# Handing five of the last fifteen pieces of a weighted sum to ScalarE and GpSimd, with one release per buffer and a last store in four parts

## What is computed

```python
topw, topi = jax.lax.top_k(scores, K)                 # K = 2 of E = 8 experts
for e in range(E):
    m = topi == e
    sel = m.any(axis=-1)
    wmean = (topw * m).sum() / jnp.maximum(cnt, 1)    # one weight per expert
    y = _mlp(xf, expert_gate_w[e], expert_up_w[e], expert_down_w[e])
    out = out + jnp.where(sel[:, None], y * wmean, 0)
out = out + _mlp(x, shared_gate_w, shared_up_w, shared_down_w)
x = x + out
```

## Time and profile before

| | |
|---|---|
| median of 3 executions | 1134.68 us |
| the three | 1134.67, 1134.68, 1140.13 us |
| the profiled execution's own time | 1135.8 us |
| its span, first to last instruction | 1134.0 us |
| granted TensorE clock over the span | 0.958 |
| PE, DVE, POOL, ACT busy | 88%, 71%, 55%, 47% |

### The profile page before, as it was taken

One profiled execution on the slowest core, in us unless ns is written; L12 is line 12 of the kernel. 1 busy time (PEld: TensorE's weight loads), 2 busy tenths in 40 slices (PEclk: granted clock), 3 DMA queues, 4 the chain that ended last, 5 costly groups with the idle time before them and its releaser, 6 DMA issues.

```text
span 1134.0 us, 26153 instructions
## 1 busy us (share of the span) xinstructions
PE 992.8 (88%) x9538; PEld 728.5 (64%) x9538; DVE 800.1 (71%) x2109; ACT 529.1 (47%) x994; POOL 623.1 (55%) x1008
## 2 busy tenths in 40 slices
PE   4799997995899899899899989989989989988991
PEld 2465657773666566676576666656667667758891
DVE  2889984474576876886767787677688676557487
ACT  3777775524324433542542533443353256745770
POOL 5469898573237447636806826744663315345561
PEclk9899998987999999999989999999999999989996
DMA  9555524253001430150151151131011264324589
GB/s 204 130 176 140 180 79 169 78 176 113 19 3 48 131 110 29 61 174 21 65 184 39 66 174 42 48 99 58 29 58 56 98 229 123 95 80 132 160 297 330
DMA packets 87100, 127.69 MB, mean 113 GB/s; under 512 B 28352, under 2 KB 62784, under 8 KB 84800
## 3 DMA queue, kind: packets, MB, share of 16 engines
q1 hardware_dynamic: 79776, 106.30, 30.1%
q0 software_dynamic: 7200, 19.74, 4.8%
HBM read 66.47 MB, written 59.55 MB: 111 GB/s over the span
## 4 chain that ended last, share of the span: by engine, by line
PE 46%; DVE 20%; POOL 18%; issue 8%; ACT 5%; DMA 2%; ACTq 0%; SPq 0%; DVEq 0%; POOLq 0%
POOL arena L1585 6%; POOL arena L1587 6%; DVE arena L1714 3%; PE bank L570 3%; PE bank L507 3%; PE bank L742 3%; PE bank L989 3%; PE bank L812 3%; POOL arena L1477 2%; PE bank L584 2%; POOL orn L1603 2%; PE bank L477 2%; PE bank L596 2%; PE bank L939 2%; DVE top L1896 2%
## 5 line engine op out<-in xcount | busy, mean ns | idle before, releaser
L1063 ACT ACTIVATE arena<-bank 128x512 f32<-128x512 f32 (+4 forms) x360 | 186.7, 539 | 336.7 <-PE bank L980 61.8
L1585 POOL TENSOR_TENSOR arena<-arena 128x126 f32<-128x126 f32 (+22 forms) x248 | 107.7, 434 | 42.3 <-DVE arena L1773 24.4
L1714 DVE SCALAR_TENSOR_TENSOR arena<-arena,param 128x512 f32<-128x512 f32 x144 | 103.8, 774 | 18.6 <-ACT arena L1087 17.9
L1647 POOL DMA_INDIRECT results<-arena x78 | 76.1, 976 | 71.1 <-DVE arena L2273 43.9
L1587 POOL TENSOR_TENSOR arena<-arena 128x126 f32<-128x126 f32 (+22 forms) x248 | 102.8, 415 | 19.4
L1556 POOL TENSOR_TENSOR arena<-arena,rb 128x256 f32<-128x256 f32 x32 | 19.8, 618 | 139.6 <-ACT arena L1063 139.2
L1532 POOL DMA_INDIRECT slots_x<-arena x64 | 63.5, 993 | 37.4 <-DVE arena L2006 21.5
L428 PE MATMUL bank<-const,arena 128*128 128x128 f32 x256 | 39.6, 305 | 49.9 <-POOL arena L1477 25.7
L989 PE MATMUL bank<-arena 128*128 128x128 f32 x624 | 82.5, 275 | 0.2 <-ACT arena L1387 0.2
L989 PEld LDWEIGHTS bank<-arena 128*128 128x128 f32 x624 | 75.9, 192 | 0.4 <-issue 0.4
L428 PEld LDWEIGHTS bank<-const,arena 128*128 128x128 f32 x256 | 32.5, 158 | 59.3 <-DVE arena L2204 25.6
(11 more groups left out here) (293 smaller groups left out, 2616.8 us busy)
## 6 DMA issues: line engine op xcount, KB each, us to landing
arena<-slots_x SPq DMA_DIRECT2D x78, 129.0 KB, 2.2
slots_x<-rows_of_no_token SPq DMA_DIRECT2D x8, 1161.0 KB, 9.3
xt<-x_in SPq DMA_DIRECT2D x16, 512.0 KB, 5.6
kq<-kq_T SPq DMA_DIRECT2D x8, 1024.0 KB, 7.5
arena<-results SPq DMA_DIRECT2D x32, 256.0 KB, 5.1
kq_T<-kq SPq DMA_DIRECT2D x7, 1024.0 KB, 3.9
arena<-ffn_in SPq DMA_DIRECT2D x7, 768.0 KB, 4.2
vT<-v_T SPq DMA_DIRECT2D x8, 514.0 KB, 4.0
```

The costliest lines, as they stand in the source:

```text
L1063: free(act.activation(out_, in_, func, **kw), name)
L1585: own.link(pool.tensor_tensor(tmp, rows32[:, m0:, k].unsqueeze(2).broadcast_to([P, nm, k]), units[:, 0:k, k].unsqueeze(1).broadcast_to([P, ...
L1647: pool.indirect_dma_start(results[:, :], bass.IndirectOffsetOnAxis(ap=dest[:, n % YS:n % YS + 1], axis=0), ys[:, n % YS, :], None).then_in ...
L1714: ins = V.scalar_tensor_tensor(cv[:, k % 4, :], pre[:, j, d:d + GT], param[:, at:at + 1], cv[:, k % 4, :], ALU.mult, ALU.add)
```

## The change

Pieces 18, 21, 24, 27 and 30 leave DVE. ACT multiplies both halves of such a piece by their weights, in place in the `gathered` buffer; GpSimd then adds both halves to the accumulator, with two plain additions. ACT does this behind all its other work, and GpSimd behind its last scatter. DVE keeps ten of the fifteen pieces behind the loop. Since pieces now end on two engines, each of the eight buffers gets a semaphore of its own (`used00` to `used13`) in place of the one counter, and the store of a group waits for four of them. DVE waits for the accumulator's load at each piece of groups 0 to 5, not at a group's first alone. The last group's store of 512 KB becomes four stores of 128 KB, each issued once its piece is done.

```diff
+POOL_PIECES = tuple(range(len(PIECES) + 1, NG * T, 3))
...
             steps(TILE0[2] + 1 - at_step[0])
+            act.wait_ge(sem("coef_ready"), 1)
+            for j in POOL_PIECES:
+                i, t = divmod(j, T)
+                act.wait_ge(sem(f"gathered{i % 2}{t}"), 16 * (i // 2 + 1))
+                for k in range(2):
+                    at = gathered[:, i % 2, t, k, :]
+                    done(act.activation(at, at, ACT.Copy, scale=coef[:, i * T + t, k:k + 1]), "scaled")
...
+            def combine(m, i, t):
+                acc = facc[i]
+                pool.wait_ge(sem("scaled"), 2 * m + 2)
+                if i < NG - 2:
+                    pool.wait_ge(sem(f"acc{i}_loaded"), 16)
+                for k in range(2):
+                    ins = pool.tensor_tensor(acc[:, t, :], acc[:, t, :], gathered[:, i % 2, t, k, :], ALU.add)
+                    if k == 0:
+                        own.link(ins)
+                    else:
+                        ins.then_inc(sem(f"used{i % 2}{t}"), 1)
...
             place(TILE0[PARTS] - placed_[0])
+            for m, j in enumerate(POOL_PIECES):
+                combine(m, *divmod(j, T))
...
-                if i < NG - 2 and t == 0:
+                if i < NG - 2:
                     dve.wait_ge(sem(f"acc{i}_loaded"), 16)
...
-                        ins.then_inc(sem("gathered_used"), 1)
+                        ins.then_inc(sem(f"used{i % 2}{t}"), 1)
...
-                    combine(*divmod(combined[0], T))
+                    if combined[0] not in POOL_PIECES:
+                        combine(*divmod(combined[0], T))
...
-                sp.wait_ge(sem("gathered_used"), (i + 1) * T)
-                sp.dma_start(out[b, g * GT:(g + 1) * GT, :].rearrange("(t p) d -> p t d", p=P),
-                             facc[i]).then_inc(sem("out_stored"), 16)
+                if i < NG - 1:
+                    for t in range(T):
+                        sp.wait_ge(sem(f"used{i % 2}{t}"), i // 2 + 1)
+                    sp.dma_start(out[b, g * GT:(g + 1) * GT, :].rearrange("(t p) d -> p t d", p=P),
+                                 facc[i]).then_inc(sem("out_stored"), 16)
+                else:
+                    for t in range(T):
+                        sp.wait_ge(sem(f"used{i % 2}{t}"), i // 2 + 1)
+                        sp.dma_start(out[b, g * GT + t * P:g * GT + (t + 1) * P, :], facc[i][:, t, :])\
+                            .then_inc(sem("out_stored"), 16)
...
-                        sp.wait_ge(sem("gathered_used"), j - 2 * T + 1)
+                        sp.wait_ge(sem(f"used{i % 2}{t}"), i // 2)
```

More of the change, by code:

```diff
@@ L2640, in _ @@
                 store_out(i)
-            sp.wait_ge(sem("out_stored"), 16 * NG)
+            sp.wait_ge(sem("out_stored"), 16 * (NG - 1 + T))
         wrong = {n: (counted.get(n), k * m) for d, m in ((PER_GROUP, NG), (PER_BATCH, B)) for n, k in d.items()
```

## The result

| | before | after |
|---|---|---|
| median, 20 executions each | 1137.3 us | 1141.57 us |
| ratio after to before | | 1.0037, 95% interval 1.002 to 1.0054 |
| own time of the profiled execution | 1135.8 us | 1140.64 us |
| its span | 1134.0 us | 1138.3 us |

The change makes the kernel slower, by 4.2 us (2.3 to 6.1). That is under the half per cent that was named, and outside the predicted range: the forecast was a gain of 0.2 us, and the range, 1133.0 to 1136.4 around a median of 1134.68, reached 1.7 us to either side. The 20 executions of the kernel before have a higher median than the 3 that the prediction had, 1137.3; so of the 7.1 us between the forecast 1134.5 and 1141.57, 2.6 lie in that base and not in the change. One execution of the change took 1426.65 us at a granted clock of 0.65 and is left out of the ratio.

The account below looks back on a forecast made before the run. Behind the loop DMA was taken as the bound, with only the last four pieces and the last store able to give time. 0 + 0 + 0.43 - 0.67 = -0.24 us took the median 1134.68 to 1134.5 us, range 1133.0 to 1136.4.

Parts of the forecast that it names:

- the last one of the sum: End of the program: the last store lands at 1133.3 and the span ends 0.5 later, at 1133.8 us.
- Loop, fetches and the added waits: Everything up to 1112.9 us stays, and the extra load and store waits cost zero.
- Pieces 18 and 21: Behind the loop: done at about 1117.1 and 1120.7, with 2.3 and 0.7 us to spare before fetches 26 and 29.
- Rival D: Fetch 26 waits for a late piece 18, delaying all behind it; slower by over half a per cent; chance 0.03.
- Pieces 24 and 27: Piece 27 done at 1127.5 instead of 1126.14; store of group 6 issued 1.3 us later, costed at nothing.
- Pieces 28 to 31: Last four pieces: piece 30 done on GpSimd at 1130.7, so they end no earlier than before.
- The last store: Four parts, the last issued at 1131.1 instead of 1130.67; issue to landing 2.2 us instead of 2.87.
- 0.5 us to the end of the span: Behind the last store's landing at 1133.3: the span ends 0.5 us later, at 1133.8.
- Rival B: DVE holds back GpSimd's additions at pieces 21 and 30; 1135.6 to 1136.3 us, milder form 1135.2; chance 0.22.
- the prediction's own signs of being wrong: Fetch 26 or 29 over 0.3 us late, additions over 0.85, DVE steps over 0.5, or DMA idle before group 6's store.
- Within half a per cent: Whole kernel: the time changes by no more than half a per cent, 5.7 us, either way; chance 0.96.
- rivals A to D: Program's end: A gain, 1133.6 us, 0.17; B slower, 1135.2 to 1136.3, 0.22; C nothing, 1134.7, 0.07; D over 0.5% slower, 0.03.

Follow-up runs that it names:

- e1: The change with no pieces on GpSimd, all fifteen on DVE; semaphores, waits and four store parts stay; ratio to the kernel before 1.0008.
- e6: Small program without the layer: 4 MB loaded and stored, one GpSimd addition, no indirect DMA; DRAIN over 0.07 us after the addition.
- the small program: Program without the layer: load 4 MB, store them, one GpSimd addition, run with 0 to 150 indirect DMAs; DRAIN over 0.07 to 5.32 us after the addition.
- e13: e3 with 5 more indirect DMAs of one column, landed before the memset; 1168.4 us, DRAIN over 8.82 us after the memset.
- e3: The kernel before plus one tiny GpSimd memset after DVE's last piece; ratio to the kernel before 1.008.
- e14: e3 with 14 more indirect DMAs of one column, landed before the memset; 1175.2 us, DRAIN over 8.90 us after the memset.
- e12: The small program with 150 indirect DMAs, all landed and the output stored before the addition; DRAIN over 3.11 us after it.

## Why the prediction was wrong

**The step that failed is the last one of the sum:** "It lands at 1133.3, the span ends 0.5 later, at 1133.8." It takes the store for the only thing that can end the program. The kernel before has a second one, GpSimd's closing, which was over at 1122.5, 11.1 us ahead of the last store's landing at 1133.6, and so didn't count. The change moves GpSimd's last instruction from 1113.84 to the last store's own time. In the trace of before the DRAIN is over 8.7 us after that instruction, so the sum was there to be made: 12.1 + 8.7 = 20.8 us after fetch 24, against 14.7 for the store, and 0.2 to the end of the span. 21.0 against 15.4 before is 5.6 us of loss instead of 0.2 of gain; measured in the profile, 21.1. I asked when an engine's last instruction ends and never what the engine still does behind it; the prediction costs the additions on POOL's queue and leaves out what is queued behind them.

Point by point:

- *Loop, fetches and the added waits, zero:* right. Fetches 28 and 30 go out 2.34 and 3.58 us after fetch 24 (2.27 and 3.58 before), and e1 shows the semaphores to be free.
- *Pieces 18 and 21, done in time:* right. ACT's scalings take 0.50 us each, predicted 0.47. Rival D's path, a late fetch 26, is out.
- *Pieces 24 and 27, the store of group 6 late by 1.3 us and free:* right, 8.93 after fetch 24 against 7.60, with the DMA share at 0.98 over it.
- *Pieces 28 to 31, "end no earlier than they did":* nearly right. The last addition is done at 12.39, predicted 12.1. The additions take 0.72 to 0.86 us each, where 0.61 and 0.2 in all had been put in. Here the row was the wrong one: the addition takes 0.72 us with DVE idle too, in the pair from 1124.52 and in e6, where nothing else runs. So 0.11 each is the size of the term, and only what is above 0.72 the conflict. DVE's waits for data grew by 2.3 us, predicted 3.
- *The last store, 2.2 us in place of 2.87:* about right as a sum. Its last part was issued 12.8 us after fetch 24, predicted 12.5, and landed 1.8 later. It landed 0.4 us earlier against fetch 24 than before, predicted 0.3. But e1, where the parts change alone, has 2.8 us, so the gain comes only where the parts have something to wait for.
- *0.5 us to the end of the span:* wrong, as said. It was 6.4.
- *Rival B, GpSimd held back by DVE:* its mechanism is there, its price is not. The rows of DVE's steps in groups 4 to 5 and 6 to 7 of the changed kernel (ns, shortest, median, longest):

```profile
L2319 DVE SCALAR_TENSOR_TENSOR arena<-arena x12: 471/485/1014, 1111.0 to 1119.1; 128x256 f32<-128x256 f32 x12
L2319 DVE SCALAR_TENSOR_TENSOR xt<-arena,xt x10: 478/485/829, 1120.5 to 1128.2; 128x256 f32<-128x256 f32 x10
```

and of GpSimd's additions:

```profile
L1653 POOL TENSOR_TENSOR xt<-xt,arena x6: 722/754/861, 1120.8 to 1128.8; 128x256 f32<-128x256 f32 x6
L1653 POOL TENSOR_TENSOR arena<-arena x4: 719/754/784, 1112.9 to 1117.6; 128x256 f32<-128x256 f32 x4
```

In the kernel before no DVE step of this stretch takes over 0.485 us; here those that begin with or during an addition take 0.74 to 1.01. (Two of the prediction's own signs of being wrong are thus met: DVE steps over 0.5 us, and one addition, 0.861, over 0.85.) A step and an addition that begin together, both at 1116.77, take 1.01 and 0.72: DVE's step comes out as its own 0.48 with 0.53 of standing still, while the addition takes what it takes alone. That is what the Trainium skill has in "SBUF — State Buffer", section "Who interferes with whom": a DVE instruction with two inputs in SBUF and a GpSimd one that reads SBUF shut each other out. The trace agrees, 0.485 to 1.01 us, which the rows of before did not show; that one side stands still for the whole of the other's instruction it shows only roughly, 0.53 of 0.72. Over the 22 steps DVE loses 2.6 us by it, 12 x (628 - 485) + 10 x (578 - 485) ns. 2.0 of it falls where DVE would wait for data. The other 0.6 falls in its last six steps, and DVE is still done 0.6 ahead of GpSimd, whose last two additions take 0.2 more in all than the prediction gave them.

**The chances.** Within half a per cent had 0.96, and that is where the time fell, but for the wrong reason: each case of the list ended on a store or a fetch, rivals A to D included. 8.7 us behind a last instruction would have been a case of the other sign with a price of its own.

Of DRAINs the Trainium skill speaks in "VectorE: DVE Perf Modes", section "The DRAIN you can't avoid": it knows two kinds, the flush behind a DVE instruction, and those at a program's beginning and end, about 12 ns on all five engines. If the closing ones here are of the second kind, SP's agrees, 13 ns in every run of the layer, and those of the other four don't, at 0.14 to 0.94 us for PE, ACT and DVE and 8.5 to 10.0 for GpSimd. The measurement decides.

## What to carry to other kernels

An engine isn't done with its last instruction: before work is moved to an engine that used to finish early, look up the closing DRAIN of each queue at the line that ends the block, and add its length behind the last instruction to the new end. On GpSimd in this program, with its 150 indirect DMAs, that was 8.4 us, so its last instruction has to lie that much ahead of the landing of the last store: by the tails, pieces up to 24 could go to GpSimd for nothing, the fourth ended the span 1.7 us later, all five 6.2. And a stretch at the end in which no engine and no DMA is busy is a closing: ask for its line, not for the engine that the wait is put down to.

## What the runs showed of the hardware

- **GpSimd's closing grows with the indirect DMAs that it has issued, not with what is in flight:** 0.07 us after the last instruction with none, then 0.16, 1.39 and 5.32 with 1, 16 and 64, which is 0.082 each. The layer has 150 and 8.4. It is about the same behind a 0.1 us memset (8.41), an addition (8.43) and a scatter (8.7 to 8.8). Beyond 64 the law is open: 3.1 with 150 in the small program, 8.4, 8.8 and 8.9 with 150, 155 and 164 in the layer.
- **A pause before the 114th:** 3.28 us in the small program with 150, where GpSimd otherwise takes up the next one after 0.30; 1.8 us of idle time at the same place in all nine profiles of the layer. What it is stays open.
- **The extra scatters of 4-byte rows held up the DMA engines.** With the five of e13, 128 rows of 4 bytes each, the memset starts 37.9 us after the last scatter of `results`, in e3 17.6. For 10 us the share of the DMA engines reads 1.25, and they move a tenth of what they did in the earlier trace rows, 38 GB/s against 395:

```profile
1130.00:1140.00 10.00, 0.00 (x0) 0.00 (x0) 0.00 (x0) 0.00 (x0) 0.00 (x0) 0.50 1.25 38
```

  Fetches of 256 KB issued from 1113 us on take 21.8 us to land, a median of 13, in the table of DMA issues of that stretch, where fetch 28 of the kernel before took 6.03:

```profile
arena<-results SPq DMA_DIRECT2D x13, 256.0 KB, 21.8
```

  So the total times of e13 and e14 say nothing on the DRAIN. The small programs issue rows of 1 KB at the same pace, and in e12 all had landed 2.5 us after the last was issued, so it is hardly the number of scatters; that it is the size of the rows was not tested by itself.
